# First layer of a two-layer graph network: each gather from the third of a group on waits for the gather two in front of it

## The reference

```
h = relu(edge_attr @ W1 + b1)
w_edge = (h @ W2 + b2).reshape(-1, 16, 16)
msgs = einsum('ei,eio->eo', x[src], w_edge)
aggr = segment_sum(msgs, dst, num_segments=n_nodes)
```

## Time and profile before

| | |
|---|---|
| median of three runs | 8242.69 us (8239.94 to 8244.3) |
| span of the profiled execution | 8221.3 us |
| the profiled execution's own time | not listed apart from the three runs |
| PE busy | 7349.2 us (89%) |
| DVE busy | 6691.0 us (81%) |
| POOL busy | 5696.0 us (69%) |
| ACT busy | 4457.4 us (54%) |
| gathers, L802 | 3,132, 971 ns of POOL each |

### The profile page before, as it was taken

How to read it: one execution, slowest core, us unless ns; L and a number is a source line. 1 busy time by engine, 2 the same in 40 slices (tenths; PEclk the granted TensorE clock), 3 DMA queues, 4 the chain that set the end, 5 groups by cost and what they waited for, 6 DMA issues and landing times. The chain is left out here.

```text
span 8221.3 us, 191064 instructions
## 1 busy us (share of the span) xinstructions
PE 7349.2 (89%) x52997; PEld 6446.6 (78%) x52997; DVE 6691.0 (81%) x17449; ACT 4457.4 (54%) x8279; POOL 5696.0 (69%) x4866
## 2 busy tenths in 40 slices
PE   7888888888888888888888886999999999999998
PEld 5667676666676666666676765999999999999996
DVE  6777777777777777777777777999999999999997
ACT  3333333333333333333333335888888878778884
POOL 6666666666666666666666664888888888888886
PEclk8999999999999999999999998999999999999999
DMA  2000000000000000000000014444444455554443
GB/s 60 18 17 17 17 17 17 17 17 17 17 17 17 17 18 17 17 17 18 17 17 17 17 23 101 73 75 74 74 75 74 74 73 74 72 74 75 73 75 64
DMA packets 713464, 341.73 MB, mean 42 GB/s; under 512 B 422115, under 2 KB 656599, under 8 KB 713427
## 3 DMA queue, kind: packets, MB, share of 16 engines
q1 hardware_dynamic: 379313, 272.94, 13.1%
q0 software_dynamic: 332928, 64.86, 12.9%
q10 hardware_dynamic: 1186, 3.51, 0.1%
HBM read 307.85 MB, written 32.96 MB: 41 GB/s over the span
## 5 line engine op out<-in xcount | busy, mean ns | idle before, releaser
L802 POOL DMA_INDIRECT xg<-gather_rows,idx x3132 | 3041.9, 971 | 1882.4 <-issue 1848.5
L919 PE MATMUL ps_w<-W2s,hT 128*128 128x256 f32 x12928 | 3240.2, 408 | 37.1 <-issue 36.6
L919 PEld LDWEIGHTS ps_w<-W2s,hT 128*128 128x128 f32 x12928 | 2678.5, 207 | 581.6 <-issue 97.0
L1745 POOL DMA_INDIRECT sums<-total,row x1616 | 2551.0, 1579 | 529.1 <-issue 474.4
L1708 PE MATMUL ps_wide<-hot_col,placed 128*128 128x392 f32 x12928 | 2434.7, 345 | 4.8 <-DVE placed L1544 2.1
L1708 PEld LDWEIGHTS ps_wide<-hot_col,placed 128*128 128x128 f32 x12928 | 2313.6, 196 | 12.2 <-issue 6.9
L841 ACT ACTIVATE hT<-ps_h,b1c 128x512 f32<-128x512 f32 x1616 | 1022.8, 680 | 2302.1 <-PE ps_h L905 2090.8
L1002 DVE TENSOR_TENSOR prod<-ps_w,xg 128x512 f32<-128x512 f32 x1616 | 1098.1, 690 | 969.7 <-remote 599.7
L1544 DVE SCALAR_TENSOR_TENSOR placed<-ps_r,src_r,halves 128x512 fp32r<-128x512 f32 x1616 | 1097.5, 741 | 0.1
L1643 ACT ACTIVATE square<-iota_col,minus_col 128x784 bf16<-128x784 int16 x1212 | 1061.3, 938 | 66.6 <-issue 58.0
L1009 DVE TENSOR_REDUCE msg<-prod 128x32 f32<-128x512 f32 x1616 | 1058.9, 676 | 0.0
(11 more groups left out here) (229 smaller groups left out, 5425.0 us busy)
## 6 DMA issues: line engine op xcount, KB each, us to landing
dst_row<-dst_rows SPq DMA_DIRECT2D x404, 256.0 KB
src_row<-src_rows SPq DMA_DIRECT2D x404, 128.0 KB
xg<-gather_rows,idx POOLq DMA_INDIRECT x3132
q_win<-q_rows SPq DMA_DIRECT2D x404, 96.0 KB
ea<-in_edge_attr SPq DMA_DIRECT2D x404, 64.0 KB
sums<-total,row POOLq DMA_INDIRECT x1616
e<-in_edge_attr SPq DMA_DIRECT2D x404, 32.0 KB
q_rows<-Q SPq DMA_DIRECT2D x12, 768.0 KB, 5.4
```

What stands on the lines that cost most here:

```text
L802: pool.indirect_dma_start(xg[r][:, t, :], None, k.rows, bass.IndirectOffsetOnAxis(ap=idx[r][:, t:t + 1], axis=0)).then_inc(xg_in[r][t], 16)
L919: last = pe.matmul(to, hT[half][:, j, col:col + P], k.W2[:, j, :], start=(j == 0), stop=(j == 1 and not with_b2))
L1745: pool.indirect_dma_start(k.sums[t], bass.IndirectOffsetOnAxis(ap=row[r][:, t:t + 1], axis=0), total[r][:, t, :], None, compute_op=ALU.add ...
```

## The change

In the loop over the tiles of a group a wait and a raise are added in front of every gather from the third on. The wait is for the landing of the gather two in front, of the same group.

```diff
                     pool.sem_inc(q["gathers_begun"], 1)
                     for t in range(T - 1 if dense(r, use) else T):
+                        if t >= 2:
+                            pool.wait_ge(xg_in[r][t - 2], 16 * (use + 1))
+                            pool.sem_inc(q["gathers_begun"], 1)
                         pool.indirect_dma_start(
                             xg[r][:, t, :], None, k.rows,
                             bass.IndirectOffsetOnAxis(ap=idx[r][:, t:t + 1], axis=0)
```

## The result

The changed kernel takes 8256.74 us (median of 20 runs, 8242.41 to 8267.95), the kernel before on the same chip 8243.11 us (20 runs, 8239.38 to 8247.07). The ratio is 1.0016, 95% interval 1.001 to 1.0022. That is 13.6 us more, less than the 0.2% that counts as no change. The forecast was 485 us more.

The account below looks back on a forecast made before the run. The first layer was taken as bound by each group's run of gathers, last landing and wake-up. 404 groups times 1.2 us added 485 us to 8242.7, giving 8728 us; range 7900 to 8970, likeliest case 8565 to 8970.

Parts of the forecast that it names:

- The period of the kernel before: First layer, per group: run of gathers 8.75 us plus last landing and wake-up 3.6 us makes 12.35 us.
- The spacing: POOL's gathers: landing 2.1 plus wake-up 0.8 us makes 2.9 us from t to t+2, where it took 2.5.
- the sum: First layer: the run's extra 1.2 us all lies on the path, over 404 groups 485 us more.
- wrong altogether: Sign in the gathers' timeline: gathers spread as computed, yet the group's period stays at 12.2 us.
- The rival of "the same": POOL's group start: released by something not moving with its gathers, idle time absorbs 1.2 us; 8243 us, chance 0.08.
- The rival of relief: First-layer gathers: pauses let the held signals through, period 11.2 us with eight gathers; 7758 us, half relief 8000; chance 0.34.
- Much slower: POOL's new waits: each also pays a 0.7 us step, making 3.6 us; 1333 us more, 9576 us; chance 0.05.

Follow-up runs that it names:

- e2: Changed kernel with distance one, each gather from the second on waiting for the one directly in front, against the kernel before: 12531.3 us, ratio 1.7156.
- e6_before: The kernel before again, unchanged, with a profile, on another chip: 7297.4 us, ratio 1.0.
- e11: The kernel before without POOL's wait for e_turned in front of a group's first gather, against the kernel before: 9182.0 us, ratio 1.117.

## Why the prediction was wrong

**The period of the kernel before** was read rightly in its numbers: run of gathers, last landing, wake-up. But the reading was too wide. I wrote that "the others' signals" get through only at the end. It is PE's raises; DVE's pass within 0.05 us in the middle of a run of the changed kernel. Nor does a raise have to wait for the last landing in general: the changed kernel's turns get through before it. And it is no property of the kernel: three of four chips of the experiments show none of it, and the same program takes 7298 to 7307 us there. The profile alone could not tell this.

**The spacing** was of the right kind and too small. The rows have pairs, 1.24 to 1.34 and then 1.77 to 1.93 us, where I had 1.25 and 1.65. t to t+2 is 1995.98 to 1999.09 and 1999.09 to 2002.24, 3.11 and 3.15 us, not 2.9; without the hold e2 has 3.14. The run grew by 1.9 us, not 1.2; from group 8 to group 400 a run of eight grew from 8.99 to 11.14 us in the mean, one of seven from 7.62 to 9.61. The medians from t to t+2 are 3.15 to 3.17 us there. The Trainium skill, "DMA: Bandwidth & Descriptors", section "Anatomy of one DMA — SWDGE (gpsimd) path", has about 2.0 us for such a DMA; the median from issue to landing is 2.4 us on the page of e6_before, so the measurement is above it, and above the 2.1 that I read on chip A.

**The step that failed** is the sum: "All of the 1.2 us lies on the path if the period is the run of gathers." It holds only while POOL, behind its last gather, waits for a held raise, and I kept that step at 3.2 to 3.6 us. I checked what the longer run adds and not what it takes away from the wait behind it. From group 8 to group 400 the mean step fell from 3.48 to 1.39 us, 2.1 us less against 2.1 us more in the run, and the period went from 12.13 to 12.14 us. (The profiled span is 27 us longer; some 4 of these are in these groups, the rest in the first eight and the last four.) Two things go with this. POOL's own chain is now the longest and PE works ahead: half of the turns end 6.9 us or more before their group starts, where it was 3.8. And the turn's raise gets through while gathers are on their way, as shown above. How much each of the two gives was not separated, and why the raise gets through is not shown. That the two sums cancel to within 0.02 us is chance. It is the case that I had named as "wrong altogether": the gathers spread out and the period stays. The rival of "the same" foresaw the result and not the cause: it had a release that doesn't move with the gathers.

**The rival of relief** was right on its mark and on part of its cause. The mark came true: the step between groups is 1.25 us (under 1.4 us in 339 of 392 groups, over 2 us in 39). The turn's raise gets through, as it said, with pauses of 1.8 to 1.9 us from start to start. The single scatter matmuls are rarer too. The row of the view of waits, 200 to 4900 us (us in total, times, longest), of before:

```profile
PE ps_a L933 <- issue: 523.5, 638, 2.7
```

and of the changed kernel:

```profile
PE ps_a L936 <- issue: 106.1, 206, 1.3
```

For `hidden`'s raise its cause did not: ACT is idle for as long as ever in front of `hT` (2302.1 us on the page of before, 2228.2 now, 858 in the changed kernel of chip C). And its price for POOL's own cycle, 11.2 us, used the 2.9 us pair; with 3.13 it is 3 x 3.13 + 2 x 1.25 = 11.9 us with eight gathers and 10.6 with seven, 11.6 in the mean. Even with the measured pair this rival would have given 0.5 x 404 = 200 us less than before, not "the same". What is missing up to 12.14 is that the means lie above the group shown: 3.2 us for t to t+2, and 1.42 for the eighth gather and 1.39 for the step between groups, where I had 1.25.

**Much slower** did not come: half of the pairs take no more than 3.2 us. One in eleven of the gathers with a wait that begin a pair starts over 2 us behind the one in front, so a few do pay.

So the equality is two limits that meet, the hold (12.2 us a group) and POOL's own chain (12.0 to 12.3 us), and that they are equal is luck. The evidence is that they move apart: take the hold away, by the chip, and the kernel before falls to 9.93 us and the changed one only to 12.03. The changed kernel takes 8131, 8146 and 8156 us on C, B and E, 101 to 126 us less than on A. That may be what the hold still costs it; the comparison is between chips, so its size was not settled.

Left open: what differs between the chips; where PE's raises wait (no view shows a raise on its way, only its maker's end and its reader's start); why the pauses let the turn's raise through and not always `hidden`'s; and whether a pause without a gather in flight, or runs of four, would free the kernel on a chip with the hold. No version beat the kernel before on any chip.

## What to carry to other kernels

A wait that is added to pace a queue costs only what it adds minus what the queue would have waited for anyway: work out the step behind it anew, with the engine that then becomes the slowest. Wait for what is far enough back: on a chip without the hold distance four cost nothing, three 0.5%, two 11.4%, one 72%. The Trainium skill, "DMA: Bandwidth & Descriptors", section "Rules for kernel authors", says for overlapping a DMA with compute to issue early and wait on its semaphore late, and these runs agree. And before an equal time is called harmless, run both kernels on another chip, at another time: the same pair gave 1.0016 on one and 1.1142 to 1.1169 on three others.

## What the runs showed of the hardware

- On two occasions of six (the result and chip D) PE's semaphore raises reached ACT or POOL late while gathers were being issued: 5.2 us from PE's end to ACT's start in e11 (gathers 1.25 us apart), 5.7 us in the changed kernel (in pairs), and in e11 PE took single steps 0.73 us apart. On the other chips the same code had ACT start behind the first matmul at once.
- It cost the kernel before some 8220 - 7298 = 922 us (chip D against C), 2.3 us a group, more than the change does anywhere.
- With gathers in pairs 3.1 to 3.2 us apart the raise of `e_turned` was taken by POOL with a gather on its way in 70 of 86 groups, with gathers 1.25 us apart in none of 193 (both on A).
- Letting POOL issue its gathers freely was no gain: without the wait for `e_turned` the kernel is equal on a chip without the hold (0.9998) and 11.7% slower with it.
- A gather's landing and POOL's restart behind it are 3.1 to 3.2 us together, on chips of both kinds.
